# A stencil layer behind an expert layer: later loads held back until the first pair has landed, and the last sum of columns made in two parts

## The chip, the core and the metric

The kernel runs on one core of a Trainium2 chip. The metric is the device time of one execution in microseconds (us); lower is better. A core has five engines with instruction queues of their own: TensorE (PE; PEld is its weight loading), VectorE (DVE), ScalarE (ACT), GpSimd (POOL) and SyncE (SP, which only issues DMAs here). 16 DMA engines move data between HBM and the on-chip memory (SBUF, 128 partitions). Engines wait for each other with semaphores; a DMA adds 16 to its semaphore when all of it has landed.

## The reference, cut to what matters

Layer 0 takes x (8 x 256 x 256, so 2048 tokens of 256), normalises it, sends each token to 2 of 8 experts and adds the two gated results to x. Layer 1 treats each of the 8 planes of 256 x 256 as a grid and applies first and second differences along rows and columns:

```python
# layer 0, its end
y = jnp.einsum('ned,ne->nd', eout, combine)   # two experts per token
x = x + y.reshape(x.shape)
# layer 1, f = x, dt one number per plane
Af = A_grid[None] * f[:, None]
Bf = B_grid[None] * f[:, None]
gradv_Af = _grad(Af[:, 0], 1) + _grad(Af[:, 1], 2)
gradvv_Bf = (_grad2(Bf[:, 0], 1) + _grad2(Bf[:, 1], 2)
             + _grad(_grad(Bf[:, 2], 2), 1) + _grad(_grad(Bf[:, 2], 1), 2))
df = -gradv_Af + gradvv_Bf * 0.5
out = jnp.maximum(f + df * dt[:, None, None], 0.0)
```

## The kernel before, in words

The expert stage (lines 397 to 910) takes the tokens sorted by expert in 23 slots. It ends at 326 us of the profile. Each slot's result is scattered to the HBM tensor `y_rows`: first the first expert's result of every token (c = 0), then the second's (c = 1). The change touches only what follows.

The stencil layer works on four pairs of planes (`NPAIR` = 4, g = 0 to 3). A pair is a tile of 128 partitions x 1024 (4 rows of 256 per partition: plane i, half q; element r = 2i + q), 512 KB. x of all planes is already in `x_sb`. Every engine runs its own list in program order:

- SyncE (lines 432 to 451) waits until every scatter has landed. It loads the first pair in halves: `Y1[0]`, `Y2[0]` for i = 0, then for i = 1, each 256 KB with a semaphore of its own (`y_first[c][i]`). Then it loads `Y1[g]` and `Y2[g]` for g = 1 to 3, 512 KB each (`y_in[c][g]`). Behind these it issues the outputs, each when ScalarE's relu is done. In the profile all `Y1` and `Y2` are named `t_y`.
- VectorE (lines 1258 to 1329) adds up the first pair itself, in `add_up`: four steps of two instructions (i = 0: x + gate * Y1, then + gate * Y2; then the same for i = 1). Then, for each pair, `center` (writes `t_kept`), `products` (eight wide products and sums, `t_b2f` to `t_qf`, and small ones for the edges) and `along_columns` (writes `t_cols`). Between pair 0 and pair 1 stands `add_second`, which adds `Y2[1]` to `x_sb`. It waits for `t_gated` = 2 and for `y1_added[1]`.
- ScalarE (lines 619 to 680) runs `keep(0)`, FD(0) (`t_fd`, the field times dt), `gated(1)`, `keep(1)`, FD(1), `keep(2)`, `relu_out(0)`, `gated(2)` and so on as line 651 has it. `gated(g)` scales `Y1[g]` and then `Y2[g]` by the gates, in place, four instructions each, and it waits for `y_in[c][g]`.
- GpSimd (lines 746 to 752) adds the gated `Y1[g]` to `x_sb` by an accumulating DMA (`y1_added[g]`), and for g = 2 and 3 also `Y2[g]`, behind the first (`y2_added[g]`).
- TensorE (lines 913 to 938) gathers each pair in two banks of PSUM: `t_kept` through the identity, `t_b0f` and `t_u` through the difference matrices, and last `t_cols` through the identity. One bank holds rows q = 0, the other q = 1. A float32 matmul is two instructions here, each with its weight load, so a pair has 4 + 8 + 8 + 4 = 24. For the last pair each bank is passed on by itself (`t_mm`), ScalarE has a relu for each and SyncE an output DMA for each.

Of the kernel before, what the change touches and what calls it, by code (L numbers as in the profile page):

```python
# [7 lines left out]
ALU = mybir.AluOpType  # L8
# [8 lines left out]
NB, T, D = 8, 256, 256  # L17
# [3 lines left out]
E, FF, TOPK = 8, 1024, 2  # L21
# [99 lines left out]
def moe_then_stencil(nc, x, ids, dt, exp_w1, exp_b1, exp_w2, exp_b2, a_grid, b_grid, small, consts, out):  # L121
# [4 lines left out]
    with ctx:  # L126
# [3 lines left out]
        def sem(name):  # L130
            return ctx.enter_context(nc.semaphore(name))
# [24 lines left out]
        with ExitStack() as phase:  # L156
            def own(name, shape, dt_=F32):
                return phase.enter_context(nc.sbuf_tensor(name, shape, dt_))
# [106 lines left out]
        with ExitStack() as phase:  # L265
            def own(name, shape, dt_=F32):
# [5 lines left out]
            FD, GG, GF, PA, PB, CC, U1, U2, PP, PQ, SM, OUT = (  # L272
                [own(f"{n}_{par}", [P, 4 * D])[:, :] for par in range(2)]
                for n in ("t_fd", "t_keep", "t_kept", "t_a0f", "t_b2f", "t_d1b2f",
                          "t_u1", "t_b0f", "t_pf", "t_qf", "t_cols", "t_out"))
# [49 lines left out]
        y_first = [[sem(f"y{c}_first{i}") for i in range(2)] for c in range(TOPK)]  # L325
        t_first = sem("t_first")
        t_f, t_u2 = sem("t_f"), sem("t_u2")
        t_u1, t_s, t_gf, t_mm, t_relu = (sem(n) for n in ("t_u1", "t_s", "t_gf", "t_mm", "t_relu"))
# [15 lines left out]
        NPAIR = NB // 2  # L344
# [31 lines left out]
        def _(sp):  # L376
# [58 lines left out]
            for i in range(2):  # L435
                for c, buf in enumerate((Y1, Y2)):
                    sp.dma_start(buf[0][:, 2 * D * i:2 * D * i + 2 * D].rearrange("p (j d) -> p j d", j=2),
                                 y_rows_tok[c, :, 2 * i:2 * i + 2, :]).then_inc(y_first[c][i], 16)
            for g in range(1, NPAIR):
                for c, buf in enumerate((Y1, Y2)):  # L440
                    sp.dma_start(buf[g].rearrange("p (j d) -> p j d", j=4),
                                 y_rows_tok[c, :, 4 * g:4 * g + 4, :]).then_inc(y_in[c][g], 16)
# [4 lines left out]
            g = NPAIR - 1  # L447
# [308 lines left out]
        def _(pe):  # L756
# [156 lines left out]
            def rows_mm(g, q, w, v, k, start=False, stop=False):  # L913
                v = v.rearrange("p (i q d) -> p q i d", i=2, q=2)
                return pe.matmul(banks[2 * g + q].rearrange("p (i d) -> p i d", i=2), w, v[:, k, :, :],  # L915
                                 start=start, stop=stop)

            def along_rows(g, col, u, start=False):
                for q in range(2):
                    for k in range(2):  # L920
                        at = col + T * k + P * q
                        rows_mm(g, q, cst[:, at:at + P], u[g % 2], k, start=start and k == 0)

            for g in range(NPAIR + 1):
                if g >= 1:
                    pe.wait_ge(t_s, g)
                    for q in range(2):
                        last = rows_mm(g - 1, q, ident, SM[(g - 1) % 2], q, stop=True)
                        if g == NPAIR or q == 1:
                            last.then_inc(t_mm, 1)  # L930
                if g < NPAIR:
                    pe.wait_ge(t_gf, g + 1)
                    for q in range(2):
                        rows_mm(g, q, ident, GF[g % 2], q, start=True)
                    pe.wait_ge(t_u2, g + 1)
                    along_rows(g, C_D2, U2)
                    pe.wait_ge(t_u1, g + 1)
                    along_rows(g, C_D1, U1)
# [3 lines left out]
        def _(dve):  # L942
# [341 lines left out]
            def rows_of(v):  # L1284
                return v.rearrange("p (r d) -> p r d", d=D)
# [31 lines left out]
            def along_columns(g):  # L1317
                par = g % 2
                pv, qv = rows_of(PP[par]), rows_of(PQ[par])
                dve.tensor_tensor(rows_of(SM[par])[:, :, 1:D - 1], pv[:, :, 2:D], qv[:, :, 0:D - 2],  # L1320
                                  ALU.add).then_inc(t_s, 1)

            add_up()
            for g in range(NPAIR):
                center(g)
                products(g)
                along_columns(g)
                if g == 0:
                    add_second()
# [21 lines left out]
```

## Time and profile before

| | us |
|---|---|
| median of 3 runs | 390.77 (389.97 to 391.19) |
| the profiled execution, its time | 391.81 |
| its span (first to last instruction) | 390.0 |
| last result of the expert stage (VectorE, ends) | 326.3 |
| last scatter landed, first load of the stencil layer issued | 329.2 |
| VectorE's four steps of `add_up` | 331.9 to 337.7 |
| last instruction of VectorE ends | 383.2 |
| last relu ends | 385.9 |
| TensorE, VectorE, ScalarE, GpSimd busy in the span | 85%, 72%, 66%, 34% |

Times inside the profile are counted from the start of the span. A wait in brackets behind a row is the time for which the engine was idle before that row, and what ended it.

### The profile page before, as it was taken

What the parts mean: (1) busy time and instruction counts of PE and PEld (TensorE: products, weight loads), DVE (VectorE), ACT (ScalarE), POOL (GpSimd) and SP (SyncE); (2) the same over time, 40 slices, a digit from 0 to 9 for tenths busy, and PEclk for the clock granted to TensorE, in tenths of its full rate; (3) what the DMA queues carried; (4) which work ended last, traced back from release to release, by engine and by line L of the source; (5) the groups of instructions that cost most, each with busy time, mean ns of one, the idle gap of its engine ahead of it and who ended that gap; (6) DMA issues with size and microseconds to landing.
All of it is one profiled execution on the core that took longest, in us unless ns stands there. A gap on an engine that the chain in (4) does not pass through costs nothing.

```text
span 390.0 us, 7285 instructions
## 1 busy us (share of the span) xinstructions
PE 329.6 (85%) x2424; PEld 298.2 (76%) x2424; DVE 279.4 (72%) x495; ACT 256.2 (66%) x467; POOL 134.3 (34%) x108
## 2 busy tenths in 40 slices
PE   1676233889999999999999999999999994299995
PEld 1565232889999999999999999999999994143331
DVE  4696772657668678768776866876876780799992
ACT  2578132577797789679769788977976851468211
POOL 1245304032425545552542454554254113011000
PEclk9998655789999999999999999999999998599999
DMA  8903352972667775874866777586587201987411
GB/s 282 323 27 104 86 208 61 337 245 70 233 226 245 269 258 179 275 219 166 284 229 206 243 269 255 189 278 198 174 284 231 77 5 61 304 201 161 108 54 55
DMA packets 49925, 74.85 MB, mean 192 GB/s; under 512 B 3309, under 2 KB 40559, under 8 KB 49776
## 3 DMA queue, kind: packets, MB, share of 16 engines
q1 hardware_dynamic: 45056, 62.13, 47.6%
q0 software_dynamic: 4512, 12.07, 11.0%
q10 hardware_dynamic: 336, 0.39, 0.3%
q8 instruction: 11, 0.18, 0.2%
q14 instruction: 10, 0.08, 0.1%
HBM read 63.56 MB, written 9.31 MB: 187 GB/s over the span
## 4 chain that ended last, share of the span: by engine, by line
PE 76%; DVE 10%; DMA 5%; ACT 4%; issue 3%; POOL 1%; SPq 0%; DVEq 0%; POOLq 0%; ACTq 0%
PE psum L866 32%; PE psum L888 29%; PE psum L915 8%; PE psum L845 2%; DMA raw_b<-in_L_cond_exp_w_dram 2%; DMA t_y<-y_rows 1%; PE psum L832 1%; PE psum L797 1%; DMA x_sb<-in_x_dram 1%; ACT relu L570 1%; POOL rs L697 1%; ACT h_pre L492 1%; DMA gathered<-h_rows,src_cur 1%; DVE st L984 1%; DVE t_b0f L1307 1%
## 5 line engine op out<-in xcount | busy, mean ns | idle before, releaser
L866 PE MATMUL psum<-slot_h,w_split 128*128 128x256 f32 (+1 forms) x1104 | 136.4, 284 | 4.4 <-DVE slot_h L1166 4.4
L866 PEld LDWEIGHTS psum<-slot_h,w_split 128*128 128x128 f32 x1104 | 134.5, 196 | 5.0 <-issue 5.0
L888 PE MATMUL psum<-w_split,hid 128*128 128x256 f32 x936 | 117.8, 285 | 0.2 <-issue 0.2
L888 PEld LDWEIGHTS psum<-w_split,hid 128*128 128x128 f32 x936 | 113.6, 192 | 0.4 <-issue 0.4
L714 POOL DMA_INDIRECT gathered<-h_rows,src_cur x40 | 58.9, 1474 | 144.0 <-DVE src_cur L1149 119.2
L570 ACT ACTIVATE relu<-psum,b_cur 128x256 f32<-128x256 f32 (+1 forms) x184 | 70.3, 446 | 19.6 <-PE psum L866 15.0
L1160 DVE TENSOR_TENSOR w_split<-raw_b,w_split 128x2048 fp32r<-128x2048 f32 x23 | 52.7, 2293 | 22.4 <-ACT w_split L552 22.4
L1154 DVE TENSOR_TENSOR w_split<-raw_a,w_split 128x2048 fp32r<-128x2048 f32 x23 | 52.6, 2288 | 19.0 <-ACT w_split L545 11.9
L1173 DVE TENSOR_TENSOR hid<-relu,hid 128x512 fp32r<-128x512 f32 (+1 forms) x92 | 53.0, 605 | 16.0 <-ACT hid L579 15.3
L727 POOL DMA_INDIRECT y_rows<-y_sb,dst_cur x39 | 53.6, 1375 | 29.2 <-DVE y_sb L1192 13.1
L545 ACT ACTIVATE w_split<-raw_a 128x2048 fp32r<-128x2048 f32 x23 | 44.2, 1922 | 27.4 <-DMA raw_a<-in_L_cond_exp_w_dram 27.3
L579 ACT ACTIVATE hid<-relu 128x512 fp32r<-128x512 f32 (+1 forms) x92 | 50.6, 584 | 0.0
L552 ACT ACTIVATE w_split<-raw_b 128x2048 fp32r<-128x2048 f32 x23 | 44.5, 1934 | 4.0 <-DMA raw_b<-in_L_cond_exp_w_dram 4.0
L1166 DVE TENSOR_TENSOR slot_h<-psum,slot_h 128x512 fp32r<-128x512 f32 (+1 forms) x23 | 14.0, 610 | 12.6 <-ACT slot_h L559 12.6
L915 PE MATMUL psum<-t_kept,cst 128*128 128x512 f32 x16 | 9.5, 724 | 13.2 <-DVE t_kept L1296 13.2
L845 PE MATMUL psum<-cst,gathered 128*128 128x128 f32 x80 | 13.3, 282 | 5.8 <-DMA gathered<-h_rows,src_cur 5.8
L797 PE MATMUL psum<-eye_rw,hT 128*128 128x136 f32 x64 | 12.6, 359 | 6.2 <-ACT hT L500 6.2
L797 PEld LDWEIGHTS psum<-eye_rw,hT 128*128 128x128 f32 x64 | 11.0, 253 | 8.0 <-ACT hT L500 6.2
L1192 DVE TENSOR_TENSOR y_sb<-psum,b_all 128x512 f32<-128x512 f32 (+1 forms) x23 | 13.6, 593 | 4.4 <-PE psum L888 4.3
L915 PEld LDWEIGHTS psum<-t_kept,cst 128*128 128x128 f32 x16 | 3.4, 223 | 17.4 <-DVE t_kept L1296 14.0
L559 ACT ACTIVATE slot_h<-psum 128x512 fp32r<-128x512 f32 (+1 forms) x23 | 12.6, 549 | 6.1 <-PE psum L845 6.1
L915 PE MATMUL psum<-t_b0f,cst 128*128 128x512 f32 x32 | 14.8, 605 | 0.9 <-DVE t_b0f L1307 0.8
(160 smaller groups left out, 271.3 us busy)
## 6 DMA issues: line engine op xcount, KB each, us to landing
raw_a<-in_L_cond_exp_w_dram SPq DMA_DIRECT2D x23, 1024.0 KB, 7.9
raw_b<-in_L_cond_exp_w_dram SPq DMA_DIRECT2D x23, 1024.0 KB, 5.7
t_y<-y_rows SPq DMA_DIRECT2D x6, 512.0 KB, 8.5
x_sb<-t_y POOLq DMA_DIRECT2D x5, 512.0 KB, 4.6
x_sb<-in_x_dram SPq DMA_DIRECT2D x4, 512.0 KB, 7.2
h_rows<-h_tok SPq DMA_DIRECT2D x16, 128.0 KB, 2.2
out_dram<-t_out SPq DMA_DIRECT2D x3, 512.0 KB, 3.0
b_all<-in_L_cond_exp_b_dram SPq DMA_DIRECT2D x1, 1024.0 KB, 10.1
```

Of the source, the lines that this page charges most:

```text
L545: act.activation(w_split[:, 0, par, 0, :], w1_raw[par], ACT.Copy).then_inc(w1_hi, 1)
L552: act.activation(w_split[:, 1, par, 0, :], w2_raw[par], ACT.Copy).then_inc(w2_hi, 1)
L570: last = act.activation(relu[:, bank, i, 0:n], banks[bank][:, ST * i:ST * i + n], ACT.Relu, bias=b1_cur[:, par, blk:blk + 1])
L579: act.activation(hid[:, par, 0, 2 * bank:2 * bank + 2, 0:n], relu[:, bank, :, 0:n], ACT.Copy).then_inc(hid_hi, 1)
L714: pool.indirect_dma_start(out=gathered[:, par, t, :], out_offset=None, in_=h_rows, in_offset=bass.IndirectOffsetOnAxis(ap=src_cur[:, par, ...
L727: pool.indirect_dma_start(out=y_rows, out_offset=bass.IndirectOffsetOnAxis(ap=dst_cur[:, par, t:t + 1], axis=0), in_=y_sb[:, par, t, :], i ...
L866: last = pe.matmul(banks[bank][:, ST * (blk % 2):ST * (blk % 2) + rows], w_split[:, 0, par, w, at:at + P], slot_h[:, par, h, k, 0:rows], s ...
L888: last = pe.matmul(banks[bank][:, D * t:D * t + D], hid[:, par, h, blk, P * t:P * t + P], w_split[:, 1, par, w, D * blk:D * blk + D], star ...
L915: return pe.matmul(banks[2 * g + q].rearrange("p (i d) -> p i d", i=2), w, v[:, k, :, :], start=start, stop=stop)
L1154: dve.tensor_tensor(w_split[:, 0, par, 1, :], w1_raw[par], w_split[:, 0, par, 0, :].bitcast(F32), ALU.subtract).then_inc(w1_lo, 1)
L1160: dve.tensor_tensor(w_split[:, 1, par, 1, :], w2_raw[par], w_split[:, 1, par, 0, :].bitcast(F32), ALU.subtract).then_inc(w2_lo, 1)
L1173: dve.tensor_tensor(hid[:, par, 1, 2 * bank:2 * bank + 2, 0:n], relu[:, bank, :, 0:n], hid[:, par, 0, 2 * bank:2 * bank + 2, 0:n].bitcast( ...
```

## The change

SyncE waits for both DMAs of the first pair's second half before it issues the loads of pairs 1 to 3. VectorE makes the last pair's `t_cols` in two instructions, one for the rows q = 0 and one for q = 1, each of half the size, and counts each on `t_s`. TensorE waits for the second count ahead of the second bank's last matmul. Pairs 0 to 2 have one `t_cols` instruction as before.

```diff
                     sp.dma_start(buf[0][:, 2 * D * i:2 * D * i + 2 * D].rearrange("p (j d) -> p j d", j=2),
                                  y_rows_tok[c, :, 2 * i:2 * i + 2, :]).then_inc(y_first[c][i], 16)
+            for c in range(TOPK):
+                sp.wait_ge(y_first[c][1], 16)
             for g in range(1, NPAIR):
                 for c, buf in enumerate((Y1, Y2)):
                     sp.dma_start(buf[g].rearrange("p (j d) -> p j d", j=4),
...
                 if g >= 1:
                     pe.wait_ge(t_s, g)
                     for q in range(2):
+                        if g == NPAIR and q == 1:
+                            pe.wait_ge(t_s, g + 1)
                         last = rows_mm(g - 1, q, ident, SM[(g - 1) % 2], q, stop=True)
                         if g == NPAIR or q == 1:
                             last.then_inc(t_mm, 1)
...
                 pv, qv = rows_of(PP[par]), rows_of(PQ[par])
-                dve.tensor_tensor(rows_of(SM[par])[:, :, 1:D - 1], pv[:, :, 2:D], qv[:, :, 0:D - 2],
-                                  ALU.add).then_inc(t_s, 1)
+                sv = rows_of(SM[par])
+                for part in ((slice(0, 4, 2), slice(1, 4, 2)) if g == NPAIR - 1 else (slice(0, 4),)):
+                    dve.tensor_tensor(sv[:, part, 1:D - 1], pv[:, part, 2:D], qv[:, part, 0:D - 2],
+                                      ALU.add).then_inc(t_s, 1)
```

## Rows read from the trace of the kernel before

**Rows 1.** The page, chain that ended last: share of the span by engine.
```profile
PE 76%; DVE 10%; DMA 5%; ACT 4%; issue 3%; POOL 1%; SPq 0%; DVEq 0%; POOLq 0%; ACTq 0%
```

**Rows 2.** The same chain in order of time: start, us, what.
```profile
330.65 5.69 DMA t_y<-y_rows
```

**Rows 3.** Timeline of VectorE: start, us, engine, line, out<-in [idle before <-releaser].
```profile
331.90 0.88 DVE L1264 SCALAR_TENSOR_TENSOR t_f<-t_y,gates,x_sb 128x256 f32<-128x256 f32 x2 [5.60 <-DMA t_y<-y_rows]
332.81 0.88 DVE L1264 SCALAR_TENSOR_TENSOR t_f<-t_y,gates,t_f 128x256 f32<-128x256 f32 x2
334.48 0.88 DVE L1264 SCALAR_TENSOR_TENSOR t_f<-t_y,gates,x_sb 128x256 f32<-128x256 f32 x2 [0.79 <-DMA t_y<-y_rows]
336.82 0.88 DVE L1264 SCALAR_TENSOR_TENSOR t_f<-t_y,gates,t_f 128x256 f32<-128x256 f32 x2 [1.46 <-DMA t_y<-y_rows]
...
348.70 1.22 DVE L1276 TENSOR_TENSOR x_sb<-x_sb,t_y 128x1024 f32<-128x1024 f32 x1
...
381.96 1.22 DVE L1320 TENSOR_TENSOR t_cols<-t_pf,t_qf 128x1016 f32<-128x1016 f32 x1
```

**Rows 4.** Timeline of SyncE's DMA issues in the stencil layer.
```profile
329.20 1.91 SPq L437 DMA_DIRECT2D t_y<-y_rows  x4
331.16 6.93 SPq L441 DMA_DIRECT2D t_y<-y_rows  x6
```

**Rows 5.** Issue to landing: line 437 all four, its first two, line 441 all six.
```profile
DMA to landing us min/median/max: 2.6/3.6/5.7
...
t_y<-y_rows SPq DMA_DIRECT2D x2, 256.0 KB, 2.8
...
DMA to landing us min/median/max: 6.7/8.5/10.0
```

**Rows 6.** Stretches: busy PE, PEld, DVE, ACT, POOL; granted clock, DMA share, GB/s.
```profile
330.00:335.00 5.00, 0.00 (x0) 0.00 (x0) 2.28 (x6) 0.72 (x1) 0.00 (x0) 0.50 0.85 250
331.00:332.00 1.00, 0.00 (x0) 0.00 (x0) 0.10 (x1) 0.00 (x0) 0.00 (x0) 0.50 1.01 320
332.00:334.00 2.00, 0.00 (x0) 0.00 (x0) 1.66 (x4) 0.27 (x1) 0.00 (x0) 0.50 0.78 230
342.00:343.00 1.00, 1.00 (x2) 0.36 (x2) 1.00 (x2) 1.00 (x3) 0.00 (x0) 0.61 1.09 350
361.17:372.13 10.96, 10.92 (x25) 4.31 (x24) 10.86 (x14) 2.36 (x3) 0.22 (x1) 1.00 0.39 96
```

**Rows 7.** The page, DMA issues: KB each, median us from issue to landing.
```profile
raw_b<-in_L_cond_exp_w_dram SPq DMA_DIRECT2D x23, 1024.0 KB, 5.7
...
out_dram<-t_out SPq DMA_DIRECT2D x3, 512.0 KB, 3.0
```

**Rows 8.** Timelines of ScalarE and GpSimd; issue to landing of line 748's first DMA.
```profile
338.36 3.29 ACT L647 ACTIVATE t_y<-t_y,gates 128x256 f32<-128x256 f32 x8
...
365.19 1.33 ACT L662 ACTIVATE t_fd<-x_sb,dt_b 128x512 f32<-128x512 f32 x2 [0.84 <-DMA x_sb<-t_y]
...
340.36 0.96 POOL L748 DMA_DIRECT2D x_sb<-t_y  x1 [12.30 <-ACT t_y L647]
...
DMA to landing us min/median/max: 7.2/7.2/7.2
```

**Rows 9.** Timeline of TensorE's matmuls, first pair and the start of the second.
```profile
346.12 3.60 PE L915 MATMUL psum<-t_u,cst 128*128 128x512 f32 x8
349.55 1.88 PE L915 MATMUL psum<-t_cols,cst 128*128 128x512 f32 x4
...
354.07 3.70 PE L915 MATMUL psum<-t_b0f,cst 128*128 128x512 f32 x8 [0.85 <-DVE t_b0f L1307]
```

**Rows 10.** TensorE's last matmuls; VectorE's 512-element sum of line 1229.
```profile
379.71 3.70 PE L915 MATMUL psum<-t_u,cst 128*128 128x512 f32 x8
383.25 1.97 PE L915 MATMUL psum<-t_cols,cst 128*128 128x512 f32 x4
...
311.15 0.68 DVE L1229 TENSOR_TENSOR gr<-grid 128x512 f32<-128x512 f32 x1
```

## The prediction, on record before the changed kernel was run

> **What bounds the kernel now.** I began with the page's chain of work that ended last: TensorE has most of it, but that is the long expert stage, which the change does not touch [rows 1]. So I read the same chain only from the end of the expert stage, in order of time. It goes through the last scatter to the DMA of the first pair's `t_y` (issued at 330.65, landed 5.69 us later, at 336.34), then through VectorE from 336.82, and in its last stretch, from 354.07, through TensorE [rows 2, 3, 9]. To see which of the two paces that stretch I looked at their busy times in one whole pair, from one `t_kept` of VectorE to the next: of 10.96 us VectorE is busy for 10.86 [rows 6]. TensorE has 24 instructions a pair, each 0.43 us behind the last where it has no wait (eight in 349.55 - 346.12 = 3.43 us), 10.3 us in all, and it waits for VectorE at 354.07 [rows 9]. (The row has TensorE busy for 10.92, since the modelled ends of its matmuls fill such gaps.) So VectorE paces the stencil layer, and its end moves with the moment at which VectorE has the first pair added up.
>
> **Part 1, the wait on SyncE: what it removes.** The four loads of the first pair (256 KB each) are issued from 329.20 to 331.11, and the six of 512 KB follow at once [rows 4]. The four land 2.6 to 5.7 us after their issue [rows 5]. VectorE's `add_up` therefore takes its four steps at 331.90, 332.81, 334.48 and 336.82: between the second and the third it waits 0.79 us, before the fourth 1.46 us [rows 3]. Is that delay due to the six loads behind? The first pair is 1.05 MB. From 330 to 335 the DMA engines moved 5 x 250 = 1250 KB [rows 6], so 0.2 MB of the later loads had moved by 335 while a piece of the first pair was still missing until 336.34; and from 332 to 334 the engines were only 78% busy, at 230 GB/s, while SyncE was pushing the later loads. Both speak for a delay by the later loads, neither proves it.
>
> With the four loads alone, when does the last one land? Bounds: the fastest of the four needed 2.6 us, so not before 330.65 + 2.6 = 333.25 [rows 5]; a weight load of 1 MB in one piece takes 5.7 us [rows 7], so from 329.20 it is there at 334.9. I take 333.9: transfers start near 330.3, and 1.05 MB at the 320 KB per us of the one undisturbed slice [rows 6] take 3.3 us, and some tenths go for the last piece. Then `add_up` runs without a wait: the fourth step starts at 331.90 plus three times 0.91 us (332.81 - 331.90) and ends 0.88 later, at 335.51 instead of 337.70. **VectorE is ready 2.19 us sooner.**
>
> **Part 1, what it adds.** Behind the new wait on SyncE stand the six loads, and behind them only the outputs, which wait for ScalarE's relus much later. Their first issue moves from 331.16 to about 333.95. Who waits for them: ScalarE's `gated(1)`, then GpSimd's accumulating DMA, then VectorE's `add_second`. Before, `gated(1)` began at 338.36, GpSimd issued 2.00 us later at 340.36, and that DMA took 7.2 us to land [rows 8]: 347.56, while VectorE came to `add_second` at 348.70 [rows 3]. So this side path had 1.14 us of slack, and `gated(1)` may begin as late as 339.50 before VectorE is later than in the kernel before.
>
> Now `gated(1)` needs Y1 of pair 1. How long does 512 KB take from a queue that is empty? Lower bound: the outputs, 3.0 us [rows 7]. Upper: the 1 MB weight load, 5.7 us. The nearest row is the start of this very stage: the first two quarters, together 512 KB, with more issued behind them, landed on average 2.8 us after issue [rows 5], the second issued 0.43 us after the first, so all of it about 3.4 us after the first issue. I take 3.6, for SyncE goes on pushing. That gives 337.55. FD(0) of ScalarE is over before (335.51 and its second half of 0.7 us), so `gated(1)` begins at 337.6, GpSimd issues at 339.6, and by the same 7.2 us the sum is at 346.8. VectorE would be at `add_second` at 348.70 - 2.19 = 346.51. So it waits about 0.3 us there: **2.19 - 0.3 = 1.9 us** are kept. The 7.2 us hold here too, I estimate, since the loads still run beneath that DMA: 3.1 MB at the 320 to 350 KB per us of the full slices [rows 6] from 335 on end near 344 to 345.
>
> The Trainium skill ("DMA: Bandwidth & Descriptors", "Anatomy of one DMA — SWDGE (gpsimd) path") gives a DMA a fixed cost of about 2.0 us beside bytes over 436 GB/s, mostly the receipt at its end; that speaks against putting two DMAs behind each other. An estimate by it is 3.2 us for 512 KB, close to the 3.4 us that the rows give, and the sum would then come out near 2.1 us; its fit was made on another queue than this one.
>
> The later users are covered. `gated(2)` comes behind `gated(1)` (3.29 us) and `keep(1)`, so not before 342, and its loads are third and fourth in the burst; `gated(3)` comes behind FD(1) and relu 0, after `add_second`, when the burst is over. The last accumulation frees ScalarE's FD(3) at 365.19 [rows 8], and VectorE asks for its result at 372.13 [rows 6]: 6.9 us of slack. Uncovered, each us of these would be one us of the end.
>
> TensorE in the first pair: it starts behind VectorE's first `t_kept`, at a granted clock of 0.50, the 1.2 GHz level, and the clock rises between 342 and 343 (0.61 in that slice) [rows 6]. If it starts 2.2 us sooner and the clock rises after the same time, nothing changes; it has 0.85 us of slack at `t_b0f` of pair 1 [rows 9].
>
> **Part 2, the sum of columns in two.** Before, VectorE's last `t_cols` runs 381.96 to 383.18 and TensorE's first matmul on it starts at 383.25 [rows 3, 10]. What does TensorE lose? Where it had no wait, the first `t_cols` matmul started 3.43 us after the first `t_u` one (349.55 - 346.12) [rows 9]. In the last pair `t_u` starts at 379.71 [rows 10], so the first possible start is 383.14, against 383.25: **0.11 us** to be had. The first half is ready at 381.96 + 0.68 (a 512-element sum) [rows 10] = 382.64. The second ends at 383.32 at the latest (another 0.68), 0.14 later than the whole did, and is wanted two instructions or 0.86 us after 383.14. Bounds: 0 to 0.11 gained; nothing is lost while that 0.86 covers it, 0.14 if it did not. The added wait on TensorE stands before a weight load; behind it is only the last bank's matmul.
>
> **The sum.** 1.9 + 0.1 = 2.0 us. The profiled execution has a span of 390.0 and a time of 391.81, 1.04 above the median of the three runs, 390.77. That execution would come to 389.8; from the median, 390.77 - 2.0 = **388.8**.
>
> **The rivals.**
> A (forecast): the delay was due to the later loads, and the side path is just late or just in time. 388.5 to 389.6 as the side path costs 0 to 1 us.
> B: the hand-over eats most of it. If the first pair lands at 334.9 as the weight load would, and pair 1's load takes 3.6 us more, `gated(1)` starts at 338.55, the sum lands at 347.75, 0.95 us before 348.70. With part 2: 389.7.
> C: the first pair does not land sooner, since the late piece is an engine's own lag and not the later loads. For: the landings of the four already spread from 2.6 to 5.7 us [rows 5], and the 1250 KB moved by 335 fit uneven engines as well. Against: the idle share while SyncE was pushing, in a queue that had work. Then the six are issued at 336.4, `gated(1)` starts at 340.0, its sum lands at 349.2: 0.5 us later than 348.70, less 0.1: 391.2. This is what the Trainium skill's rule would make of it ("DMA: Bandwidth & Descriptors", "Queues, rings and completion order": each engine takes descriptors in ring order): loads queued behind cannot hold up those ahead.
> D, the other side: the refill is slow. From the point at which the first pair's landing plus the flight of pair 1's load passes 339.5, VectorE waits at `add_second` longer than it gained. With 334.9 and 5.7 us (the weight load) to 6.7 us (the fastest of the six now) it is 340.65 to 341.65: 1.15 to 2.15 us late, less the 0.1 of part 2, 391.8 to 392.8. For: with a queue ahead none of the six took less than 6.7 us [rows 5]. Against: the queue is now empty, and the first half MB needed 3.4.
> That the wait does nothing, because the issue was past anyway, is excluded: SyncE ended the issue of the six only at 338.09 [rows 4], 4 us behind the point where the wait ends.
>
> **How the numbers follow.** A 0.57, B 0.18, C 0.15, D 0.10. Predicted 388.8; A's own range 388.3 to 389.6. The range over A, B and most of C, with 0.4 us for the scatter of a median, is 388.1 to 391.2. What a measurement of this kernel can tell is about 0.3%, 1.2 us. Faster by more than that: A, and a small share of B: 0.60. Within: most of B, all of C, the mild end of D: 0.32. Slower: the rest of D: 0.08.
>
> **What would show it.** Right: `add_up` in four steps without a wait, ending near 335.5; the six loads issued near 334; `gated(1)` at 337 to 338; VectorE idle under 1 us before `add_second`; 10.96 us for each pair after that; the first half of `t_cols` done before the last `t_u` matmul. Wrong: the fourth step still at 336 or later (C), or over 2 us of idle time before `add_second` (D).

## The result, and the profile after

| | before | after |
|---|---|---|
| median of 22 runs, us | 390.57 | 391.72 |
| ratio after to before | | 1.0041 (95%: 1.0024 to 1.0058) |
| profiled execution: time, span | 391.81, 390.0 | 391.24, 389.1 |
| SyncE's first `t_y` issue to the end of the last relu, in the profile | 56.65 | 57.66 |

The change makes the kernel slower by 0.41%, 1.6 us (the medians lie 1.15 us apart, the means 1.6). 388.8 was forecast, with a range from 388.1 to 391.2, so the prediction was wrong in its direction and missed its range. The two profiled executions seem to say the opposite, for the span of after is shorter. But from the last relu to the end of the span it is 4.1 us in the first profile of before and 2.7 in every other one, and the expert stage ended at another moment in each profile. I therefore compare profiles by the **stage**: from the first `t_y` issue of SyncE to the end of ScalarE's last relu. It is 1.0 us longer after the change.

The chain of after, in order of time (start, us, what), takes another way than the one of before [rows 2]. It goes over the side path:

```profile
330.20 4.47 DMA t_y<-y_rows
...
334.73 4.78 DMA t_y<-y_rows
...
339.54 1.72 ACT t_y L649 x4
...
341.56 7.70 DMA x_sb<-t_y
...
349.36 1.24 DVE x_sb L1280
```

Read from above: the first pair's last load; the refill, Y1 of pair 1; its gates on ScalarE; the accumulating DMA; and only then `add_second` on VectorE. Four steps stand one behind the other where before VectorE's work alone set the time.

The timeline of VectorE in after (compare [rows 3]) and, under it, of ScalarE, GpSimd and SyncE (compare [rows 4, 8]):

```profile
331.58 0.88 DVE L1268 SCALAR_TENSOR_TENSOR t_f<-t_y,gates,x_sb 128x256 f32<-128x256 f32 x2 [5.72 <-DMA t_y<-y_rows]
332.50 0.88 DVE L1268 SCALAR_TENSOR_TENSOR t_f<-t_y,gates,t_f 128x256 f32<-128x256 f32 x2
334.00 0.88 DVE L1268 SCALAR_TENSOR_TENSOR t_f<-t_y,gates,x_sb 128x256 f32<-128x256 f32 x2 [0.62 <-DMA t_y<-y_rows]
335.15 0.88 DVE L1268 SCALAR_TENSOR_TENSOR t_f<-t_y,gates,t_f 128x256 f32<-128x256 f32 x2 [0.27 <-DVE t_f L1268]
...
349.36 1.23 DVE L1280 TENSOR_TENSOR x_sb<-x_sb,t_y 128x1024 f32<-128x1024 f32 x1 [2.23 <-DMA x_sb<-t_y]
...
361.82 1.22 DVE L1300 TENSOR_TENSOR t_kept<-t_keep,x_sb 128x1024 f32<-128x1024 f32 x1
...
372.79 1.22 DVE L1300 TENSOR_TENSOR t_kept<-t_keep,x_sb 128x1024 f32<-128x1024 f32 x1
...
382.62 1.28 DVE L1326 TENSOR_TENSOR t_cols<-t_pf,t_qf 128x508 f32<-128x508 f32 x2
```

```profile
339.54 3.30 ACT L649 ACTIVATE t_y<-t_y,gates 128x256 f32<-128x256 f32 x8 [2.75 <-DMA t_y<-y_rows]
...
341.56 0.96 POOL L750 DMA_DIRECT2D x_sb<-t_y  x1 [13.94 <-ACT t_y L649]
...
328.76 1.91 SPq L437 DMA_DIRECT2D t_y<-y_rows  x4
334.73 5.02 SPq L443 DMA_DIRECT2D t_y<-y_rows  x6
...
DMA to landing us min/median/max: 7.7/7.7/7.7
```

Counted from SyncE's first issue, `add_up` ended at 8.49 us before and ends at 7.27 after (335.15 + 0.88 - 328.76): 1.2 us won. `gated(1)` began at 9.16 and begins at 10.78. VectorE then stands idle for 2.23 us at `add_second`, which began at 19.50 and begins at 20.60: 1.1 us lost. From there on everything is as before: a pair still takes 10.97 us (372.79 - 361.82). The bracket of the fourth step names VectorE itself, but the step follows the landing: it began 0.48 us behind it in after (5.91 and 6.39 us from the first issue), as it did before (7.13 and 7.62).

### The profile page after: what moved, and what is told of

It reads as the page before. It is cut to its first block, busy times and chain, and to the rows that moved or that the text cites. A ratio compares the mean times of both kernels' runs of the same rounds, so it can differ in the third digit from the quotient of the medians.

```text
span 389.1 us, 7287 instructions
## 1 busy us (share of the span) xinstructions
PE 328.9 (85%) x2424; PEld 297.6 (76%) x2424; DVE 279.5 (72%) x496; ACT 255.8 (66%) x467; POOL 137.8 (35%) x108
## 4 chain that ended last, share of the span: by engine, by line
PE 77%; DVE 8%; DMA 7%; ACT 3%; issue 2%; POOL 2%; SPq 0%; DVEq 0%; POOLq 0%; ACTq 0%
PE psum L868 34%; PE psum L890 29%; PE psum L917 8%; DMA t_y<-y_rows 2%; PE psum L847 2%; DMA x_sb<-t_y 2%; PE psum L834 1%; POOL rs L703 1%; DVE st L988 1%; DMA x_sb<-in_x_dram 1%; POOL rs L699 1%; DMA gathered<-h_rows,src_cur 1%; PE psum L787 1%; DMA y_rows<-y_sb,dst_cur 1%; ACT h_pre L494 0%
## 5 line engine op out<-in xcount | busy, mean ns | idle before, releaser
L716 POOL DMA_INDIRECT gathered<-h_rows,src_cur x40 | 60.3, 1508 | 142.2 <-DVE src_cur L1153 93.0
L729 POOL DMA_INDIRECT y_rows<-y_sb,dst_cur x39 | 55.8, 1430 | 27.1 <-DVE y_sb L1196 12.5
L799 PE MATMUL psum<-eye_rw,hT 128*128 128x136 f32 x64 | 11.5, 331 | 6.7 <-ACT hT L502 6.6
L799 PEld LDWEIGHTS psum<-eye_rw,hT 128*128 128x128 f32 x64 | 9.7, 225 | 8.6 <-ACT hT L502 6.7
```

The costliest lines, as they stand in the source:

```text
L716: pool.indirect_dma_start(out=gathered[:, par, t, :], out_offset=None, in_=h_rows, in_offset=bass.IndirectOffsetOnAxis(ap=src_cur[:, par, ...
L729: pool.indirect_dma_start(out=y_rows, out_offset=bass.IndirectOffsetOnAxis(ap=dst_cur[:, par, t:t + 1], axis=0), in_=y_sb[:, par, t, :], i ...
```

## The experiments

All numbers of the tables are us from SyncE's first `t_y` issue, taken from one profile of each kernel; where a profile was taken again, it has a row of its own. "4th" is the landing of the first pair's fourth load, "accumulate" the time from issue to landing of GpSimd's DMA of Y1 of pair 1, "idle" VectorE's idle time before `add_second`. Ratios are against runs of before on the same chip.

### First: which part costs, and through what

a1_hold_only: the wait on SyncE without the two-part sum (the edit against the kernel before; the edits below are against the changed kernel).

```diff
+            for c in range(TOPK):
+                sp.wait_ge(y_first[c][1], 16)
```

> The wait on SyncE alone, the sum of columns whole. Measure: the stage, from SyncE's first t_y issue to the end of ScalarE's last relu (56.65 us before, 57.66 us in the changed kernel). Theory S (the side path Y1 of pair 1, gates, accumulating DMA is late): 57.6 to 57.9 us, ScalarE's gated(1) waits 2 to 3 us for its load, VectorE waits 1.5 to 3 us before add_second, time about 0.3 to 0.5% above before. Rival T (the two-part sum costs the time, by its extra wait on TensorE): stage at or under 56.7 us, time as before or below.

a2_split_only: the two-part sum without the wait.

```diff
-            for c in range(TOPK):
-                sp.wait_ge(y_first[c][1], 16)
```

> The two-part sum alone, no wait on SyncE. Theory S: the stage is 56.5 to 56.65 us (0.0 to 0.11 us gained), the time can't be told from before. Rival T: stage near 57.6 us and the time 0.3 to 0.5% above before.

a3_y1_ahead: only Y1 of pair 1 is issued ahead of the wait.

```diff
-            for c in range(TOPK):
-                sp.wait_ge(y_first[c][1], 16)
             for g in range(1, NPAIR):
                 for c, buf in enumerate((Y1, Y2)):
+                    if (g, c) == (1, 1):
+                        for n in range(TOPK):
+                            sp.wait_ge(y_first[n][1], 16)
```

> The changed kernel, but the load of Y1 of pair 1 is issued ahead of SyncE's wait; the other five stay behind it. Theory S: the first pair lands as in the changed kernel or up to 0.5 us later, gated(1) begins 7.5 to 8.3 us after SyncE's first issue (9.2 before, 10.8 in the changed kernel), VectorE waits under 0.5 us before add_second, stage 54.8 to 55.7 us, time 0.2 to 0.5% below before. Rival R (any load behind the first pair delays it as before): add_up ends 8.3 to 8.6 us after the first issue as before, stage 56.4 to 56.8 us. Rival L (the accumulating DMA takes over 8 us whenever the burst starts late, whoever feeds it): VectorE waits over 1 us before add_second and the stage is 56 us or more.

a4_no_side: the changed kernel without the side path.

```diff
-            for g in range(1, NPAIR):
+            for g in range(2, NPAIR):
                 pool.wait_ge(t_gated, 2 * g - 1)
...
-                dve.wait_ge(y1_added[1], 16)
```

> The changed kernel without the accumulating DMA of Y1 of pair 1 and without VectorE's wait for it; left out of the computation: Y1 of pair 1 is not added. Theory S: VectorE's 2.2 to 2.4 us of idle time before add_second are gone and the stage falls by as much, to 55.2 to 55.5 us, time 0.2 to 0.4% below before. Rival (the stage is longer for another reason, TensorE or the outputs): it falls by under 1 us.

| | 4th | `add_up` ends | `gated(1)` | accumulate | idle | `add_second` | stage | ratio (95%) |
|---|---|---|---|---|---|---|---|---|
| before | 7.13 | 8.49 | 9.16 | 7.2 | 0 | 19.50 | 56.65 | |
| after | 5.91 | 7.27 | 10.78 | 7.7 | 2.23 | 20.60 | 57.66 | 1.0041 (1.0024 to 1.0058) |
| a1_hold_only | 5.91 | 7.26 | 10.57 | 7.7 | 2.0 | 20.39 | 57.55 | 1.0020 (0.9997 to 1.0042) |
| a2_split_only | 6.21 | 7.57 | 8.53 | 7.6 | 0 | 18.58 | 55.63 | 0.9993 (0.9968 to 1.0019) |
| a3_y1_ahead | 6.47 | 7.83 | 8.49 | 8.9 | 0.54 | 19.45 | 56.51 | 1.0001 (0.9984 to 1.0019) |
| a4_no_side | 5.93 | 7.29 | 9.99 | none | 0 | 18.29 | 55.35 | 0.9991 (0.9971 to 1.0011) |

The wait alone gives the stage of the changed kernel. Its ratio, 1.0020, was expected at 1.003 to 1.005; its interval (0.9997 to 1.0042) takes in most of that and also no change. The two-part sum does no harm. Without the side path the idle time is gone, and the stage is 2.3 us shorter than after: the loss goes through the side path and nowhere else.

The run that upset my sum is a2_split_only. I had expected a stage of 56.5 to 56.65 us, and it has 55.63, although it issues its loads just as before does. Its fourth load landed after 6.21 us, not 7.13. So had I built the forecast on a late landing? And a3 is a miss: its stage is 56.51 us where at most 55.7 was expected, and its time is that of before. Its refill is early, `gated(1)` at 8.49, but its fourth load lands at 6.47 and the accumulating DMA takes 8.9 us, so the gain is lost again (rival L in part; the idle time is 0.54 us, not over 1).

### Second: was the first profile of before a late draw?

A draw is what one execution happens to have of a time that scatters from one execution to the next.

before_again and before_third are the kernel before, after_again is the changed kernel, all unchanged; b1_before_no_side makes the edit of a4 in the kernel before.

> The kernel before, unchanged, profiled again. In the first profile of before the fourth load of the first pair landed 7.13 us after SyncE's first issue; in the split-only run, whose loads are issued in the same way, after 6.21. Theory O (the first profile was a late draw): the landing is at 6.0 to 6.6 us here and the stage 55.6 to 56.0 us. Theory N (7.1 us is what before has): 7.0 us or more, stage 56.5 or more.

> The changed kernel profiled again. Theory S (side path late): the fourth load lands 5.8 to 6.0 us after the first issue, gated(1) begins at 10 to 11 us, VectorE waits 1.5 to 2.5 us before add_second, stage 56.9 to 57.8 us. If the first profile of it was a late draw too, the wait before add_second is under 1 us.

> The kernel before without the accumulating DMA of Y1 of pair 1 and VectorE's wait for it; left out of the computation: Y1 of pair 1 is not added. Theory S: the side path is hidden here, so the stage is that of before for the same landing of the fourth load, add_second 10.97 to 11.05 us behind the end of add_up and no more than 0.1 us of idle time. Against the same edit in the changed kernel (stage 55.35 us) it shows what holding the loads back gives by itself: 0.2 to 0.5 us. Rival (my first sum): the fourth load lands over 7 us and the difference is 1 us or more.

> The kernel before a third time. With nothing held back the fourth load of the first pair has landed 7.13, 6.91, 6.47 (one load behind), 6.21 and 5.96 us after SyncE's first issue; held back, 5.69 to 5.93. Theory O2 (the six loads behind add 0 to 1.3 us to it, by chance): between 5.9 and 7.2 us, VectorE's add_second without idle time, the stage 55.5 to 56.7 us. Against it: a landing over 7.3 us, or idle time of VectorE before add_second.

| | 4th | `add_up` ends | `gated(1)` | accumulate | idle | `add_second` | stage |
|---|---|---|---|---|---|---|---|
| before_again | 6.91 | 8.27 | 8.93 | 7.2 | 0 | 19.27 | 56.42 |
| before_third | 5.93 | 7.29 | 8.51 | 8.0 | 0.19 | 18.57 | 55.71 |
| b1_before_no_side | 5.96 | 7.32 | 7.98 | none | 0 | 18.32 | 55.47 |
| after_again | 5.69 | 7.05 | 10.54 | 8.1 | 2.63 | 20.76 | 57.83 |

VectorE's third and fourth step in before_third, and `add_second`:

```profile
333.55 0.88 DVE L1264 SCALAR_TENSOR_TENSOR t_f<-t_y,gates,x_sb 128x256 f32<-128x256 f32 x2 [0.25 <-DMA t_y<-y_rows]
335.06 0.88 DVE L1264 SCALAR_TENSOR_TENSOR t_f<-t_y,gates,t_f 128x256 f32<-128x256 f32 x2 [0.63 <-DMA t_y<-y_rows]
...
347.22 1.23 DVE L1276 TENSOR_TENSOR x_sb<-x_sb,t_y 128x1024 f32<-128x1024 f32 x1 [0.19 <-DMA x_sb<-t_y]
```

With the loads issued at once the fourth lands anywhere from 5.93 to 7.13 us, and `add_up` ends at 7.29 to 8.49, on average 7.88 over six profiles (8.49, 8.27, 7.29, 7.57, 7.32, and 8.34 in f1 below). Held back, it ends at 7.05 to 7.35, on average 7.22 over nine. So the later loads do delay the first pair, but by 0 to 1.2 us and 0.66 on average. Theory O was wrong for before_again (6.91 lies between the two theories' ranges, near 7.13) and right for before_third: one profile did not show what is typical, and neither would the second. It is a scatter between executions and not between chips only: before_again (6.91) and b1 (5.96) ran on one chip. after_again had 0.13 us more idle time than expected. b1 missed its last figure: against a4 (55.35 us) its stage is 0.12 us longer, 0.1 of it the two-part sum, where 0.2 to 0.5 was expected for holding the loads back. With a fourth load that lands at 5.96 anyway, there is nothing to gain. The last row of the fence shows something else: the side path is not safely hidden in the kernel before either. When the first pair is early, `add_second` already waits 0.19 us for it.

`add_second` begins on average at 18.98 with the loads at once (19.50, 19.27, 18.57, 18.58) and at 20.58 held back (20.60, 20.76, 20.39): 1.6 us later, less 0.1 for the two-part sum. These 1.5 us are 0.38% of the time, beside the 0.41% measured (0.24 to 0.58).

### Third: why the side path is late

b3_wait_first_halves: SyncE waits only for the first half's two loads.

```diff
             for c in range(TOPK):
-                sp.wait_ge(y_first[c][1], 16)
+                sp.wait_ge(y_first[c][0], 16)
```

> The changed kernel, but SyncE waits only for the two loads of the first half (landed after about 3.5 us). Theory S: the six are issued from 3.5 us on, while the third and fourth loads are under way and the queue never runs empty, so gated(1) begins at 8.3 to 9.3 us as before, VectorE waits under 0.8 us before add_second and the stage is 55.4 to 56.7 us. Rival (any wait of SyncE costs, whenever it ends): gated(1) at 10 us or later and the stage over 57 us.

d2_from_x: the first pair's loads read x.

```diff
-                                 y_rows_tok[c, :, 2 * i:2 * i + 2, :]).then_inc(y_first[c][i], 16)
+                                 x_tok[:, 4 * c + 2 * i:4 * c + 2 * i + 2, :]).then_inc(y_first[c][i], 16)
```

> The changed kernel with the first pair's four loads taken from the input x instead of y_rows; same shapes, 1 KB rows. Left out: the expert results of pair 0, other numbers stand in their place. Theory Q (1 MB into an empty queue needs this long, whatever it reads): the four land at 2.6 to 2.9, 3.3 to 3.6, 4.9 to 5.3 and 5.6 to 6.0 us after the first issue, as in the changed kernel. Rival W (rows just scattered are slow to read): the third at under 4.5 and the fourth at under 5.2 us.

e1_one_by_one: Y1 of pair 1 has landed before the other five are issued.

```diff
                 for c, buf in enumerate((Y1, Y2)):
+                    if (g, c) == (1, 1):
+                        sp.wait_ge(y_in[0][1], 16)
```

> The changed kernel with one wait more on SyncE: after the load of Y1 of pair 1 it waits until that has landed before it issues the other five. Theory U (the refill takes 4.0 to 4.8 us since the five others are pushed in behind it and run ahead on some engines): Y1 of pair 1 lands 3.0 to 3.7 us after its issue and gated(1) begins at 9.0 to 9.5 us. Rival V (512 KB into an empty queue takes 4 us or more by itself): it lands 4.0 us or more after its issue, gated(1) at 9.9 us or later. The rest of the burst comes later in both.

c2_hold_pair3_too: pair 3's loads wait for ScalarE.

```diff
             for g in range(1, NPAIR):
+                if g == 3:
+                    sp.wait_ge(t_gated, 2)
```

> The changed kernel with a second wait on SyncE: the two loads of pair 3 are issued only when ScalarE has gated pair 1 (t_gated = 2). Nothing is left out. Theory B (the accumulating DMA takes 7.7 us since the burst runs beneath it): it lands 5.0 to 6.5 us after its issue, VectorE's wait before add_second falls from 2.2 to 0 to 1 us, stage 55.4 to 56.5 us. Rival (it takes 7 us or more for a reason of its own): the wait stays near 2 us and the stage near 57.5 us. A wait of ScalarE for pair 3's loads would show at gated(3).

| | 4th | SyncE goes on | `gated(1)` | accumulate | idle | `add_second` | stage |
|---|---|---|---|---|---|---|---|
| b3_wait_first_halves | 5.91 | 3.45 | 9.34 | 8.2 | 1.29 | 19.64 | 56.70 |
| d2_from_x | 5.75 | 5.81 | 10.70 | 7.9 | 2.47 | 20.67 | 57.72 |
| e1_one_by_one | 5.97 | 6.03 | 10.67 | 10.0 | 4.34 | 22.76 | 60.10 |
| c2_hold_pair3_too | 5.70 | 5.76 | 10.51 | 5.7 | 0.22 | 18.36 | 55.42 |

Three facts come out. **The first pair alone needs 5.7 to 6.0 us**, whatever it reads: from x the four land at 2.75, 3.49, 5.05 and 5.75, as in after (theory Q). After the second landing (3.45 us after the first issue in after, at 332.21) the queue slows down without any load behind; stretches of after (last two columns: DMA share, GB/s):

```profile
330.00:331.00 1.00, 0.00 (x0) 0.00 (x0) 0.00 (x0) 0.00 (x0) 0.00 (x0) 0.50 0.76 267
...
332.00:333.00 1.00, 0.00 (x0) 0.00 (x0) 0.96 (x4) 0.00 (x0) 0.00 (x0) 0.50 0.66 183
333.00:334.00 1.00, 0.00 (x0) 0.00 (x0) 0.38 (x1) 0.58 (x1) 0.00 (x0) 0.50 0.87 304
...
331.56:333.56 2.00, 0.00 (x0) 0.00 (x0) 1.76 (x4) 0.14 (x1) 0.00 (x0) 0.50 0.78 218
```

The 78% of [rows 6] that I had laid to the pushing of the later loads is there without them. The last row is the same stretch of after, 2.8 to 4.8 us from the first issue, and it has 78% too. Over this stretch the nine profiles with the loads held back have 73 to 89%, the six with the loads at once 78 to 93%. That was my main witness, and it was none.

**A refill of 512 KB into the empty queue takes 4.0 to 4.9 us by itself.** In e1 nothing is pushed behind it until it has landed, and SyncE's issue at 336.32 still lands after 4.6 us, against 4.8 in after:

```profile
t_y<-y_rows SPq DMA_DIRECT2D x1, 512.0 KB, 4.6
```

Rival V holds. Where in these 4.6 us the time goes, when the stage's first two loads of 256 KB took 3.4 together, stays open.

**The accumulating DMA takes longer the more of the burst runs beneath it.** In c2 pair 3's 1 MB is issued only at 13.83 us, 1.3 us behind that DMA, and the DMA lands after 5.7 us, not 7.7. VectorE's and GpSimd's rows of c2, and that DMA:

```profile
342.60 0.96 POOL L752 DMA_DIRECT2D x_sb<-t_y  x1 [13.67 <-ACT t_y L651]
...
348.44 1.22 DVE L1282 TENSOR_TENSOR x_sb<-x_sb,t_y 128x1024 f32<-128x1024 f32 x1 [0.22 <-DMA x_sb<-t_y]
...
DMA to landing us min/median/max: 5.7/5.7/5.7
```

`gated(1)` is as late as in after (10.51), and still the idle time falls from 2.2 to 0.22 us. Compare e1: there the burst is latest, and the DMA takes 10.0 us. b3 was expected to keep the queue from running empty and the idle time under 0.8 us; it had 1.29. Its refill came at 9.32, in time by 1 us, but the DMA took 8.2 us. Its fourth load landed at 5.91, although the six were issued from 3.45 on.

### Fourth: a version meant to keep the gain

c3_halves is c2 with Y1 of pair 1 in two DMAs of 256 KB. f2_halves_again is the same kernel on another chip. f1_only_pair3_held has the second wait without the first.

```diff
+                    if (c, g) == (0, 1):
+                        for i in range(2):
+                            sp.dma_start(buf[g][:, 2 * D * i:2 * D * i + 2 * D].rearrange("p (j d) -> p j d", j=2),
+                                         y_rows_tok[c, :, 4 + 2 * i:6 + 2 * i, :]).then_inc(y_in[c][g], 16)
+                        continue
...
-                    act.wait_ge(y_in[c][g], 16)
+                    act.wait_ge(y_in[c][g], 32 if (c, g) == (0, 1) else 16)
```

> The second hold-back (pair 3's loads behind gated(1)) and Y1 of pair 1 loaded as two DMAs of 256 KB into the then empty queue. Theory H (one DMA of 512 KB into an empty queue is slow in itself, two of 256 KB are not: 4.0 to 4.8 us against 3.3 to 3.6): gated(1) begins 3.5 to 4.0 us after the wait on SyncE ends, that is at 9.2 to 9.8 us instead of 10.5, the 0.2 us of VectorE's idle time before add_second are gone, stage 55.2 to 55.5 us, time 0.0 to 0.25% below before. Rival: gated(1) at 10.3 us or later, as with one DMA.

> The version with both waits and Y1 of pair 1 in two DMAs again, beside the one with the second wait alone on the same chip. It was 0.28% below before (0.13 to 0.43) although its profiled stage, 56.04 us, was not short. If that was its true place: 0.15 to 0.4% below before again. If it was the draw of that chip: the interval takes in no change, and it does not differ from the version with the second wait alone.

```diff
-            for c in range(TOPK):
-                sp.wait_ge(y_first[c][1], 16)
             for g in range(1, NPAIR):
+                if g == 3:
+                    sp.wait_ge(t_gated, 2)
```

> The two-part sum, no wait for the first pair, but the two loads of pair 3 are issued only when ScalarE has gated pair 1 (t_gated = 2). Theory B (what makes the side path long is the burst beneath the accumulating DMA, and the first wait is of no use): gated(1) at 8.0 to 9.2 us, the accumulating DMA lands 4.6 to 6.5 us after its issue, no idle time before add_second, stage 55.4 to 56.5 us (set by the fourth load alone), time 0 to 0.2% below before. Rival (the first wait gives as much as it costs once the burst is short): stage over 56.5 us and slower than the version with both waits by 0.2% or more.

| | 4th | `add_up` ends | `gated(1)` | accumulate | idle | `add_second` | stage | ratio (95%) |
|---|---|---|---|---|---|---|---|---|
| c2_hold_pair3_too | 5.70 | 7.06 | 10.51 | 5.7 | 0.22 | 18.36 | 55.42 | 0.9996 (0.9971 to 1.0020) |
| c3_halves | 5.99 | 7.35 | 10.92 | 6.0 | 0.56 | 19.00 | 56.04 | 0.9972 (0.9957 to 0.9987) |
| f2_halves_again | 5.89 | 7.25 | 10.83 | 5.5 | 0 | 18.43 | 55.48 | 0.9970 (0.9950 to 0.9991) |
| f1_only_pair3_held | 6.98 | 8.34 | 9.00 | 5.7 | 0 | 19.34 | 56.39 | 1.0001 (0.9975 to 1.0026) |

f2's rows, with the refill in halves at 335.98 and `add_second` without a wait:

```profile
335.98 0.88 SPq L447 DMA_DIRECT2D t_y<-y_rows  x2
...
340.86 1.71 ACT L656 ACTIVATE t_y<-t_y,gates 128x256 f32<-128x256 f32 x4 [2.83 <-DMA t_y<-y_rows]
...
348.46 1.22 DVE L1287 TENSOR_TENSOR x_sb<-x_sb,t_y 128x1024 f32<-128x1024 f32 x1
```

The halves did not do what they were made for: `gated(1)` begins 4.9 us after the wait ends, no earlier than with one DMA, so theory H is refuted. Yet the kernel is faster than before on two chips, by 0.28% and 0.30%, intervals without 1 in them, and so, by the sum of the two ratios and not by a run of both together, by about 0.7% faster than the changed kernel. Why it is faster is shown only in part. The gain of the first wait (0.66 us on average) without the cost of the side path points the same way, but its two stages (56.04 and 55.48) are on average 0.5 us under the three of before (56.65, 56.42, 55.71). That is 0.13%, the least that the first interval allows and half of what was measured. c2, with the same two waits, has a stage of 55.42 and an interval that takes in both no change and that gain; whether the halves add anything can't be told. Nor can f1 be told from before or from f2 by its ratio. In its profile the fourth load is late again (6.98), and the short accumulating DMA has nothing to save: without the first wait the side path was as good as hidden anyway (0.19 us in before_third was the most).

## Why the prediction was wrong, point by point

**VectorE paces the stage: right.** After `add_second` every pair takes 10.97 us in both kernels, and the end moves with that moment. From `add_second` to the end of the last relu it is 37.14 to 37.16 us in every profile with the sum whole, 37.04 to 37.07 with the sum in two parts, wherever `add_second` began. Only e1 has 37.34: TensorE stood idle for 3.3 us before its second pair (from 352.3 to 355.6), the granted clock fell to 0.50 meanwhile (0.92 in the slice 354 to 355) and stayed there from 355 to 361. In after TensorE was idle there for 2.6 us, and the clock is 1.00 from 354 to 361.

**When the first pair lands alone: the step that failed first.** I took 4.7 us after the first issue (333.9 - 329.20), from the fastest slice, 320 KB per us held for 3.3 us. It was 5.91. The bound that I had from the weight load, 1 MB in 5.7 us [rows 7], was near it: it is a whole transfer of this size, with all that happens in it, while one full slice is only its best part. With it (5.7, then 0.48 to VectorE's step as before, then 0.88 for the step) `add_up` would have ended 1.4 us sooner, not 2.19. Nor did the four steps run without a wait: VectorE still waits 0.62 and 0.27 us before the third and the fourth.

**What the later loads do to it: mis-sized by the choice of execution.** My sum stood on one profile in which the fourth load landed after 7.13 us, the latest of the six with all loads issued at once. The average gain is 0.66 us, not 1.2 and not 2.19. Of the two witnesses (1250 KB moved by 335, engines 78% busy) the second is refuted above. Rival C, that the late piece is an engine's own lag, holds in part: in three of the six profiles of loads issued at once the landing (5.93, 5.96, 6.21) is that of the loads held back, or near it. The trace has the 16 additions to a load's semaphore one by one. Of the fourth load's, in before 15 had come by 6.06 us and the last at 7.13, and in f1 by 6.11 and at 6.98, while with the loads held back the last is never more than 0.4 us behind the one before it. In before_again, though, the last five are spread from 6.00 to 6.91. So a single late piece makes most of the delay in two of the three late profiles, and the fourth load has such a piece only with loads behind it; how those cause it is open. The Trainium skill's rule ("DMA: Bandwidth & Descriptors", "Queues, rings and completion order"), that an engine takes descriptors in ring order, agrees with the landings of 5.93 to 5.96 us with six loads behind them, and by itself does not explain those of 6.9 to 7.1. The same section adds that a later descriptor may finish its write before an earlier one, so my conclusion that loads behind cannot hold up those ahead went further than the page.

**The refill: 3.6 us forecast, 4.78 measured,** and 4.0 to 4.9 in all profiles with the wait. I took the nearest row, two DMAs of 256 KB at the start of the stage, and left the upper bound of 5.7 to a rival. By the Trainium skill's figures the estimate was 3.2 us ("DMA: Bandwidth & Descriptors", "Anatomy of one DMA — SWDGE (gpsimd) path"), further off still; the measurement decides. (With 3.2 us nothing would be left of the 0.3 us of waiting, and the sum would be 2.3 us, not the 2.1 that stands there.) The chain of after has the three DMAs one behind the other, as the warning drawn from that section has it; how much of each is a fixed part no run here shows.

**The accumulating DMA: 7.2 us forecast, 7.7 and 8.1 measured.** I argued that it stays since the burst would still run beneath it. The burst ran longer instead: its last load landed 18.96 us after the first issue, before 16.0. I had let it end by 345 without adding the pause of the queue to it. Part of this is scatter as well: in before_third, with nothing held back, the last load landed at 18.66 and the DMA took 8.0 us. On average it took 7.5 us with the loads at once (four profiles) and 7.8 held back (after, a1, after_again, d2).

**The sum of the side path.** Forecast: landing at 346.8 - 329.20 = 17.6 us after the first issue. Measured: 5.97 (SyncE goes on) + 4.78 (refill) + 2.05 (to GpSimd's issue) + 7.70 (accumulating DMA) = 20.50. Of the 2.9 us too many 1.2 come from the first pair, 1.2 from the refill, 0.5 from the accumulating DMA. The slack was 1.14 us.

**The rivals.** D named the place and the point: from `gated(1)` at 339.5, that is 10.30 after the first issue, VectorE loses. It began at 10.78, and 0.5 us beyond that point plus 0.5 of the accumulating DMA is the 1.1 us lost in the profile. Its price, 391.8 to 392.8, was missed by 0.1 only (391.72), but partly by luck: of its two terms the first pair's (334.9, that is 5.7 us) was nearly right, while the refill took 4.8 us and not 5.7 to 6.7, and the accumulating DMA, which D left at 7.2, made up for some of that. D had 0.10, since I asked of it both upper bounds at once; something between the forecast and D, with a slow first pair and a refill of 4.8 us, had no rival of its own. And its place should have been read once more with another early landing of the first pair in mind: the slack of 1.14 us was that of a late draw. In before_third it is gone.

**Part 2: right, 0.1 us.** It is the difference of the two distances just named; a1 alone has 37.16, a2 alone 37.05. The two halves take 1.28 us together, 0.06 more than the whole. At the last weight loads of after TensorE does not wait beyond its own pace, 0.24 us between two weight loads: not at the first for `t_cols` (before it had stood idle there for 0.65 us), and not at the third, which stands behind the added wait:

```profile
383.48 0.19 PEld L917 LDWEIGHTS psum<-t_cols,cst 128*128 128x128 f32 x1 [0.24 <-DVE t_cols L1326]
383.91 0.19 PEld L917 LDWEIGHTS psum<-t_cols,cst 128*128 128x128 f32 x1 [0.24 <-issue]
384.34 0.19 PEld L917 LDWEIGHTS psum<-t_cols,cst 128*128 128x128 f32 x1 [0.24 <-issue]
```

**TensorE's clock and the later users: right.** Counted from SyncE's first issue, TensorE's first matmul came 1.2 us sooner (337.34 - 328.76 against 339.01 - 329.20). The granted clock, 0.50 until then, was 0.92 in the slice 340 to 341 and full behind it, and TensorE waits 0.85 us at `t_b0f` of pair 1 as before. That it rises after the same time did not hold, and did not matter: in after_again TensorE began as early (337.05) and the clock was 0.50 until the slice 343 to 344 (0.93), and from `add_second` to the last relu it is 37.06 us there too.

## What to carry to other kernels

Holding a load back until another has landed empties the queue: count the way of the held load from the issue to its last user with whole transfers of that size, not with the best slice of a burst, and set that against the slack of the path that it feeds. Take that slack, and the delay to be cured, from several profiles; a landing at the end of a burst here scatters by 1.2 us, as much as the whole effect. If something must be held back, hold back what is needed last (pair 3 here): it shortens the burst beneath everything that is needed first (the accumulating DMA took 5.5 to 6.0 us in all four profiles with it). By itself it gained nothing that could be measured here (f1, 1.0001).

## What the runs showed of the hardware

- Four loads of 256 KB alone in the queue land at 2.6 to 2.8, 3.3 to 3.6, 5.0 to 5.3 and 5.7 to 6.0 us after the first issue: between the second and the third lie 1.6 to 1.9 us, between the others 0.7 to 0.9. In after the engines are only 66% busy from 332 to 333, between the two landings, with no load but these in flight. The gap is the same when the rows come from another tensor (1.56 us in d2). What makes this gap is open.
- A load of 512 KB into an empty queue took 4.6 us with nothing behind it, 4.0 to 4.9 with others behind, and as much in two DMAs as in one.
- An accumulating DMA of 512 KB from GpSimd lands after 4.5 to 4.6 us with at most an output beside it (line 754 of after, both DMAs; the engines are then fully busy at 197 GB/s in the slices 363 to 365, while the full slices of the loads have 320 to 350 [rows 6]), 5.5 to 6.0 beside a short burst, 7.2 to 8.9 beside the long one and 10.0 beside the latest.
- The granted clock fell back to 0.50 once within the stencil layer, in e1, while TensorE stood idle for 3.3 us; behind the 2.6 us of idle time in after it was 1.00.
- A time as small as 0.1 us shows cleanly in distances inside a profile (37.15 against 37.05), where the ratio of whole runs can't tell 0.2%.
